# Two window-attention stages made one stream of 32 tiles each, and two expert stages reordered

## The reference, cut to what matters

```python
# window attention, DEPTH = 2 layers, HEADS = 8, DIM_HEAD = 64, WINDOW = 64
h = shift_token(x)                       # the upper 64 channels come from the token before
q, k, v = split(h @ wqkv)
q, k = l2norm(q) * qs, l2norm(k) * ks
q, k = rotary_xpos(q, k)                 # multiply by cos and sin tables
x = x + local_attention(q, k, v) @ wo    # each window of 64 sees itself and the one before
h = shift_token(x)
h = (h - mean(h)) / sqrt(var(h) + 1e-5) * lg + lb
a, g = split(h @ w1 + b1)                # 341 wide each
x = x + (a * gelu(g)) @ w2 + b2

# experts: groups of 32 tokens, 128 expert slots
logits = einsum('bntd,des->bntes', grouped, Wc) + bc + tie
perm   = (logits == max over the 32 tokens)          # each slot takes one token of a group
inner  = relu(permuted @ W1 + b1)                    # each slot has its own 128 x 32
out    = (inner @ W2 + b2), put back by perm
```

## Time and profile before

| | us |
|---|---|
| median of 3 runs | 2715.95 (2713.83 to 2716.72) |
| the profiled execution, its own time | 2716.01 |
| its span in the profile | 2714.2 |
| first window stage (377.7 to 795.3) | 417.6 |
| second window stage (837.0 to 1252.7) | 415.7 |
| first expert stage (2302.0 to 2399.5) | 97.5 |
| second expert stage, from 2607.9 to its last addition at 2705.6 | 97.7 |

### The profile page before, as it was taken

How to read it: one execution, slowest core, us unless ns; L and a number is a source line. 1 busy time by engine, 2 the same in 40 slices (tenths; PEclk the granted TensorE clock), 3 DMA queues, 4 the chain that set the end, 5 groups by cost and what they waited for, 6 DMA issues and landing times. The chain is left out here.

```text
span 2714.2 us, 42839 instructions
## 1 busy us (share of the span) xinstructions
PE 2225.2 (82%) x15196; PEld 1524.2 (56%) x15196; DVE 1772.0 (65%) x4423; ACT 1385.8 (51%) x3630; POOL 718.8 (26%) x472
## 2 busy tenths in 40 slices
PE   6999979889887987978447887768776988689978
PEld 4888846636643653653347774433424765556648
DVE  6777748759746965964656663356456997637863
ACT  3555537738734764864411226563636764326750
POOL 0000016516502642630033420000012976051000
PEclk9999999989988989999678898888987999778986
DMA  1000021100002101001012320000001221100010
GB/s 56 14 19 15 7 72 22 23 20 21 21 5 75 25 17 24 21 16 48 0 36 58 74 46 0 12 12 6 4 12 56 86 70 60 45 10 2 2 65 17
DMA packets 79043, 80.92 MB, mean 30 GB/s; under 512 B 28624, under 2 KB 63952, under 8 KB 77808
## 3 DMA queue, kind: packets, MB, share of 16 engines
q1 hardware_dynamic: 78832, 78.19, 10.1%
HBM read 53.94 MB, written 8.52 MB: 23 GB/s over the span
## 5 line engine op out<-in xcount | busy, mean ns | idle before, releaser
L1014 ACT ACTIVATE window_s<-window_s,window_soft 128x128 f32<-128x128 f32 x512 | 197.7, 394 | 5.0 <-DVE window_soft L1177 5.0
L1084 POOL TENSOR_TENSOR window_s<-window_s,window_soft 128x512 f32<-128x512 f32 x128 | 133.2, 1041 | 218.5 <-DVE window_soft L1114 218.4
L1092 POOL TENSOR_TENSOR window_pa<-window_pa,window_pb 128x1024 f32<-128x1024 f32 x64 | 151.5, 2368 | 148.8 <-DVE window_pb L1159 148.8
L1177 DVE CUSTOM_DVE_ANT_0 window_s<-ps,window_mask,window_nrn 128x128 f32<-128x128 f32 x512 | 148.7, 346 | 46.7 <-PE ps L859 29.9
L3127 DVE TENSOR_TENSOR_SCAN mamba_bx<-ps,mamba_ab 128x256 f32<-128x256 f32 x256 | 154.5, 667 | 18.9 <-PE ps L2913 18.9
L822 PE MATMUL ps<-window_wa,window_sh 128*128 128x512 f32 x256 | 131.3, 638 | 41.4 <-DVE window_pb L1159 28.4
L3297 ACT ACTIVATE rope_p<-ps,rope_mx 128x128 f32<-128x128 f32 (+1 forms) x256 | 104.3, 419 | 53.1 <-DVE rope_mx L3351 53.1
L2910 PE MATMUL ps<-mamba_m,mamba_xt 128*128 128x129 f32 x512 | 102.9, 283 | 29.6 <-ACT mamba_m L2985 20.6
L83 PE MATMUL ps<-x,consts 128*128 128x512 f32 x120 | 77.0, 801 | 46.1 <-PEq L53 40.5
L3015 POOL TENSOR_TENSOR h<-mamba_bx,mamba_cbr 128x1024 f32<-128x1024 f32 x32 | 89.3, 2796 | 93.2 <-DVE mamba_bx L3127 92.7
L2910 PEld LDWEIGHTS ps<-mamba_m,mamba_xt 128*128 128x128 f32 x512 | 82.3, 197 | 49.1 <-issue 49.1
(11 more groups left out here) (607 smaller groups left out, 6235.9 us busy)
## 6 DMA issues: line engine op xcount, KB each, us to landing
mamba_cbr<-mamba_c SPq DMA_DIRECT2D x32, 512.0 KB, 3.7
window_vs<-window_vt SPq DMA_DIRECT2D x64, 128.0 KB, 2.3
delta_xi<-delta_x SPq DMA_DIRECT2D x16, 512.0 KB, 5.1
switch_w<-in_switch_w SPq DMA_DIRECT2D x4, 2048.0 KB, 10.1
window_wa<-in_window_wa SPq DMA_DIRECT2D x4, 1152.0 KB, 6.8
linattn_wb<-in_linattn_wb SPq DMA_DIRECT2D x6, 513.0 KB, 3.5
window_wb<-in_window_wb SPq DMA_DIRECT2D x4, 537.5 KB, 7.7
window_sh<-y SPq DMA_DIRECT2D x16, 128.0 KB, 2.2
```

The source lines that it names most:

```text
L1014: a = nc.scalar.activation(s[:, k % 2, e, c, :], s[:, k % 2, e, c, :], ACT.Exp, scale=-1.0, bias=soft[:, k % 2, e, 1, c:c + 1], accum_out= ...
L1084: nc.gpsimd.tensor_tensor(s[:, k % 2, e], s[:, k % 2, e], soft[:, k % 2, e, 3, :].unsqueeze(2).to_broadcast([P, QC, P]), ALU.mult)\
L1092: nc.gpsimd.tensor_tensor(own, own, pb[:, :, :, :].rearrange("p a h d -> p (a h d)"), ALU.add)\
L1177: v = nc.vector.tensor_tensor_reduce(s[:, k % 2, e, c, :], K.ps[:, B_S + e, toks(c, P)], mask[:, k % 2, :], nrn[:, k % 4, h:h + 1], 3e38, ...
```

## The change

Attention. The 2 x 16 tiles of both layers become one stream of `N` = 32 tiles in `SLOTS` = 42 steps. The second half of a layer is divided into single uses of a bank, and each use is put into a step. `part(i)` says which: from step 8 on, r = (i - 8) mod 4 is the place in a block's cycle, b the block whose cycle it is (0 to 7 over both layers), and last = b - 1. Bank `B_V` is used once more in each step between the copy of v and the next v (`early`, and `mean` at r = 0), and `B_S` between the mask of one tile and the scores of the next (`late`). A block's two gate parts are first copied with their bias (`move_gate`), then one gelu of 1024 columns takes both; the third part has its gelu straight from PSUM. The table for gelu is loaded before and the one for exp and ln after it, once for each block (17 loads a stage, where it was 4). The shifts by DMA (`sh`, `sh2`) follow the blocks. The final block alone still writes its shifted copy by VectorE.

Experts. `z` is stored with the slot innermost. The picks come as eight units of 8 matmuls whose two banks are copied by ScalarE and VectorE side by side; the bias and the tie are added in one VectorE operation from PSUM; the copies of the transposed choice move to ScalarE; W1's moving operand becomes `z[:, :, 4q + r]`, with a step of 128 elements between its columns. In the combination the roles are exchanged: the choice (128 x 32) is the stationary operand and the result (128 columns) moves; b2 is added by four matmuls for each block; the result has tokens on the partitions and is copied (`y_tm`) and transposed back (`turn_back`). The three activities are interleaved by block.

```diff
+    N, BLOCKS = DEPTH * TILES, DEPTH * NJ
+    SLOTS = N + 10
+    FIRST = 2 * TPW
+    def part(i):
+        b, r = divmod(i - FIRST, TPW)
+        return (b if 0 <= b < BLOCKS else None), (b - 1 if 1 <= b <= BLOCKS else None), r
...
+            def early_moved(i):
+                b, last, r = part(i)
+                if r == 0 and last is not None:
+                    pe.wait_ge(st.hid_done, 3 * last + 2)
+                if r == 1 and b is not None:
+                    pe.wait_ge(st.log_ready, b + 1)
+                if r >= 2 and b is not None:
+                    pe.wait_ge(st.g_moved, 3 * b + 2 * r - 3)
...
+            def early(i):
+                b, last, r = part(i)
+                pe.wait_ge(st.v_copied, up_to(i))
...
+                if r == 0 and last is not None:
+                    hidden(last, 1)
+                if r == 1 and b is not None:
+                    var(b)
+                if r == 2 and b is not None:
+                    gate(b, 0)
+                if r == 3 and b is not None:
+                    gate(b, 2)
+
+            def late(i):
...
+                if r == 0 and last is not None:
+                    hidden(last, 2)
+                if r == 1 and last is not None:
+                    mlp_out(last)
+                if r == 2 and b is not None:
+                    gate(b, 1)
+                if r == 3 and b is not None:
+                    hidden(b, 0)
...
+            for i in stream:
+                b, last, r = part(i)
+                if 2 <= i < N + 2:
+                    turn_qk(i - 2)
+                if i < N:
+                    project_qk(i)
+                if i >= FIRST:
+                    early(i)
+                if 2 <= i < N + 2:
+                    scores(i - 2)
+                if 4 <= i < N + 4:
+                    project_out(i - 4)
+                if r == 0 and b is not None:
+                    early_moved(i)
+                    mean(b)
+                if 3 <= i < N + 3:
+                    turn_p(i - 3)
+                if i < N:
+                    project_v(i)
+                if i >= FIRST:
+                    late(i)
+                if 3 <= i < N + 3:
+                    values(i - 3)
...
+            def gelus(b):
+                m = HC[2][1]
+                act.wait_ge(st.hid_g, 3 * b + 3)
+                if b >= 1:
+                    act.wait_ge(st.hid_done, 3 * b)
+                nc.scalar.activation(gl[0:m, 2, :], K.ps[0:m, B_V, :], ACT.Gelu, bias=b1g(b // NJ, 2))\
+                    .then_inc(st.g_moved, 1)
+                act.wait_ge(st.g_moved, 3 * b + 2)
+                nc.scalar.activation(gl[:, 0:2, :], gl[:, 0:2, :], ACT.Gelu).then_inc(st.gelu_done, 1)
+                nc.scalar.preload_act_table_set("natural_log_exp_and_others")
...
-    z = st.sb("z", [P, ES, NG])
+    z = st.sb("z", [P, NG, ES])
...
+            def combine(j):
+                bank = K.ps[:, 4 + j % 2, :]
+                if j >= 2:
+                    pe.wait_ge(st.y_copied, j - 1)
+                for t in range(TPW):
+                    nc.tensor.matmul(bank[:, toks(t, P)], perm[:, toks(TPW * j + t, P)], b2, start=(t == 0), stop=False,
+                                     skip_group_check=True)
+                pe.wait_ge(st.moved_act, 2 * (j + 1))
+                pe.wait_ge(st.moved_dve, 2 * (j + 1))
+                for t in range(TPW):
+                    for g in range(4):
+                        n = 4 * (TPW * j + t) + g
+                        mm = nc.tensor.matmul(K.ps[32 * g:32 * g + 32, 4 + j % 2, toks(t, P)], perm[:, toks(n, GT)],
+                                              resm[:, n, :], start=False, stop=True, skip_group_check=True)
+                mm.then_inc(st.y_ready, 1)
```

More of the change, by code:

```diff
@@ new lines, in _ @@
+            for i in stream:
+                b, last, r = part(i)
+                if 3 <= i < N + 3:
+                    exps(i - 3, 1)
+                if 2 <= i < N + 2:
+                    move_qk(i - 2)
+                if 1 <= i < N + 1:
+                    inverse(i - 1)
+                if i < N:
+                    square(i)
+                if r == 1 and b is not None:
+                    rstd(b)
+                if r == 2 and b is not None:
+                    move_gate(b, 0)
+                if r == 3 and b is not None:
+                    gelus(b)
+                if 3 <= i < N + 3:
+                    move_p(i - 3)
+                if 2 <= i < N + 2:
+                    exps(i - 2, 0)
+                if r == 0 and b is not None:
+                    centered_square(b)
+                if r == 2 and b is not None:
+                    move_gate(b, 1)
@@ new lines, in _ @@
+            for i in stream:
+                b, last, r = part(i)
+                if 4 <= i < N + 4:
+                    move_o(i - 4)
+                if 3 <= i < N + 3:
+                    recip(i - 3, 0)
+                if 1 <= i < N + 1:
+                    move_v(i - 1)
+                    norms(i - 1)
+                if 3 <= i < N + 3:
+                    recip(i - 3, 1)
+                if 2 <= i < N + 2:
+                    negate(i - 2)
+                    mask_and_max(i - 2, 0)
+                if r == 0 and last is not None:
+                    gated(last, 1)
+                if 4 <= i < N + 4:
+                    attended(i - 4)
+                if i < N:
+                    cosines(i)
+                if r == 0 and b is not None:
+                    centre(b)
+                if 2 <= i < N + 2:
+                    mask_and_max(i - 2, 1)
+                if i < N:
+                    sines(i)
+                if r == 0 and last is not None:
+                    gated(last, 2)
+                if r == 1 and b is not None:
+                    normalise(b)
+                if r == 1 and last is not None:
+                    finish(last)
+                if r == 3 and b is not None:
+                    gated(b, 0)
@@ new lines, in pick @@
+            def pick(j, u):
+                pe.wait_ge(st.chosen_copied, j + 1)
+                if u:
+                    pe.wait_ge(st.picked_act, seen[j, 0])
+                    pe.wait_ge(st.picked_dve, seen[j, 0])
+                for t in range(TPW):
+                    for e in range(2):
+                        g = 2 * u + e
+                        rows, tile = slice(32 * g, 32 * g + 32), toks(TPW * j + t, P)
+                        mm = nc.tensor.matmul(K.ps[:, j + 4 * e, toks(t, P)], h_tm[rows, tile], perm_tm[rows, tile],
+                                              start=True, stop=True)
+                mm.then_inc(st.picked, 1)
@@ L3516, in _ @@
                             mm.then_inc(st.h2_ready, 1)
[L3517 to L3530 removed]
+            turn_result(0)
```

579 lines of the change are left out of this document (265 added, 314 removed).

## The result

The changed kernel takes 2595.57 us (median, 2594.42 to 2599.26); the kernel before, run again beside it, took 2714.89. The ratio is 0.9563, 95% interval 0.9546 to 0.9580. The forecast of 2585 lies 11 us too low.

A forecast was written before the change was run, and what follows sets the result against it. TensorE (PE) was to become the bound, where a loop over PE and ACT closed the steps. Window stages -75.7 and expert stages -55.6 sum to -131.3 from 2716.0, so 2584.7 us; range 2550 to 2630.

The forecast's parts named there:

- The walk of the four steps: Attention stream, one block: steps r = 0 to 3 of 11.35, 10.9, 9.1, 11.1 us; taken as 43.0, bounds 40 and 46.
- Rival 1: PE's order hides the waits: a block 40 us, expert stages give 34 each, 2538 us; below 2550, chance 0.10.
- rival 2: Bank uses in the stream serialise, each waiting for its reader: 12 us a step, +60, 2645 us; above 2630, chance 0.12.
- rival 4: TensorE falls to 1.2 GHz inside the stream: 38.6 us more for each such block; chance 0.02.
- rival 3: Table loads hold ScalarE longer than their own 1.28 us, lengthening r = 3: +41, 2626 us; chance 0.03.
- The stage's sum: One window stage: 76.1 + 39.6 + 215.0 + 10.5 + 37.6 = 378.8 us; both stages together minus 75.7.
- the 2.8 us: Window stage's start: first shift of y no longer waits for the last of four normalisations, 78.9 to 76.1 us.
- (a): Expert picks: two units side by side, copies 0.6 to 0.66 us, W1 beginning at 2326.7: minus 14.9 us a stage.
- DVE's queue sets the end: Expert picks: four `choose` of 2.1 us until 2321.2, then seven copies of 0.75 us, ending at 2326.5.
- (b): W1 in an expert stage: moving operand stepping 512 bytes costs +1 us on 5.86, between no cost and +5.9.
- (c): Expert stage's end, transposes and combination: 35.5 us falls to 21.6, minus 13.9.
- rival 5: Expert part fails by itself (W1 twice as long, the end at the low clock): +25, 2610 us; no chance given.

The follow-up runs named there:

- gating_before_mask: The changed kernel with VectorE doing gated(last, 1) before its first mask in steps r = 0, not after it: 2587.82 us, ratio 0.9526 to the kernel before.
- no_table_switch: The changed kernel with both gelus replaced by copies with and without bias, so the table loads fall out (output lacks the gelu): 2581.53 us, ratio 0.9503.
- expert_part_only: The kernel before with only the new expert stages (`switch_stage`), window stages as before: 2666.99 us, ratio 0.9820.
- mlp_out_one_product: The changed kernel with one of the three `mlp_out` products kept in r = 1 (two hidden parts left out): 2583.62 us, ratio 0.9514.
- both_steps_padded: The changed kernel with `z` rows of 130 (520 bytes) and results in rows of 65 (transpose weights step 260 bytes): 2595.26 us, ratio 0.9556.

## Why the prediction was right, and where it was off

**The walk of the four steps.** Predicted 11.35, 10.9, 9.1 and 11.1 from scores to scores, taken as 43.0 a block; measured 11.68, 11.06, 9.46 and 10.72, 42.9 (by the copies of v 11.68, 11.19, 9.32 and 10.72). Rival 1 (waits hidden, 40) and rival 2 (uses serialise, 12 us a step) fell by this, and rival 4 by the clock of 1.00 in the stream. The steps were right in their causes also. r = 0 waited for the gating: `gating_before_mask` took the wait away. It is smaller than drawn (0.9 us of TensorE, not the 1.1 from 2.0 to 3.1), and behind it stood the centring. r = 1 is TensorE alone, as said: it is busy all of the 11.06 us. "If `finish` came 2 us later, `v_copied` would hold the gate" was too generous: `finish` ended 7.8 us after the scores, as walked (8.0), but the copy of the output, a reciprocal and the copy of v itself follow, and `v_copied` came 1.04 us before it was needed. r = 3 was over-priced by 0.4.

**The table loads.** The row of 1.28 us back to back held in the new place: 1.28, gelu 0.02 later, 0.02 from the second gelu to the second load, 0.01 from its end to the copy. The Trainium skill's page "ScalarE: Activation LUTs", section "What ACT_TABLE_LOAD costs", adds about 1380 ns of drain to a switch; no such gap is in these rows, and rival 3 fell. The page's advice to batch by set (section "Table sets: the hidden batching unit") still has a price here: 1.38 us a block. Not 16 blocks pay it: from the scores of step 8 to those of the last tile a stage lost 8.0 us, and the chain at its end, which had a stretch at the lower clock in this run, got no shorter. So it is 16 us by the steps, and 14 by the medians (no_table_switch 2581.5, the change 2595.6).

**The stage's sum.** 380.7 and 379.5 for 378.8, by terms (both stages, from scores to scores): the start 78.5 and 77.3 for 76.1, the first block 39.9 and 39.9 for 39.6, the five full blocks 214.0 and 214.0 for 215.0, step 32 10.4 for 10.5, the chain at the end 37.9 for 37.6. The start is the term that was mis-sized. The first copy of v came 1.3 us earlier, nearer the first stage's start, but most of the lead was gone at the next one (7.48 us later, where it had been 6.55; here a stretch at the lower clock lay from 396.9 to 403.7, before from 390.2 to 397.0). From the stage's start to the copy of tile 7 it was 77.1 us for 77.4 before, and in the second stage 75.9 for 76.5. Of the 2.8 us 0.3 and 0.6 were left. Even these can't be told from chance: in other traces the same code took 75.7 to 79.0 for this stretch, and the code of before 76.4 to 79.8.

**The expert stages.** Predicted -27.8 each, measured -18.0 and -24.6. (a) The picks: W1 began 10.1 us earlier in the first stage and 14.7 in the second, for 14.9. The copies were 0.60 and 0.69 side by side as said, so the failed part is "DVE's queue sets the end". The last units, first stage:

```profile
2249.44 6.07 PE L3536 MATMUL ps<-ln_xc,ln_sq 32*128 32x128 f32 x64
...
2255.54 0.60 ACT L3617 ACTIVATE switch_z<-ps 128x512 f32<-128x512 f32 x1 [1.33 <-PE ps L3536]
2255.54 0.69 DVE L3677 COPY switch_z<-ps 128x512 f32<-128x512 f32 x1 [1.23 <-PE ps L3536]
```

Both copying engines wait for TensorE, at a clock of 0.55. Four units take 6.07 us, 1.5 each, where I let copies of 0.75 set the pace. Part of that is not the clock. Before, the products of four row groups of 32 stood side by side in TensorE's order; four records, one for each row group, then came every 0.21 us at the lower clock and every 0.11 at the higher. A unit has two row groups, and mostly only two records come in the same 0.21 or 0.11. A set of 32 records at the lower clock before, for comparison:

```profile
2332.64 2.09 PE L3494 MATMUL ps<-ln_xc,ln_sq 32*128 32x128 f32 x32 [3.12 <-DVE switch_z L3453]
```

The prediction has no term for TensorE in the picks, and no run prices this pairing alone. In the second stage the picks lay at the higher clock; the last copies began 25.7 us after the stage's start, not 28.6, and the gain is nearly the predicted one.

(b) W1 is the step that failed: "between no cost and twice its length (+5.9) I take +1", by the ratio of the transposes whose weights step 256 bytes. It measured 12.5 us, +6.7 in the first stage and outside the bound, and 10.2, +4.3, in the second; in four other kernels the same code took 10.2 to 10.9, inside the bound. A ratio for weights that step 256 bytes said nothing of a moving operand that steps 512. With 516 bytes my +1 would have been +1.9. I had "W1's moving operand at several times its time" as a sign of being wrong; it was about twice.

(c) The end took 22.0 us (from the first transpose to the last addition) for 21.6, at a clock of 0.91: right, and -13.5 for -13.9; 21.8 in the second stage.

Together: the window stages gave 2.6 us less than forecast, the expert stages 13.0 less, and the untouched stretches returned 4.3 that nobody had forecast: 2.6 + 13.0 - 4.3 = 11.3, the distance from 2584.7 to the profiled execution (span 2594.2 and 1.8 around it). That the untouched stages took 4.3 off the miss is luck. Of rival 5 (expert part fails by itself, 2610) half came true, by its first cause.

What stays open: why the same stretches differ between the traced executions, and how VectorE comes to be slow beside W1. Adds over 0.7 us came only with a step of 512 bytes: there the first add of a stage took 0.77 to 2.83 us, and in the first stage here the next two 1.58 and 1.14, while with 516 or 520 bytes and contiguous all took 0.68 to 0.69. The lower clock isn't needed, since the 1.58 and the 1.14 lie wholly at the higher one; which of the two memories is contended isn't shown. Nor was the exchange of roles in the combination tried by itself, so what of the 13.5 us is the exchange, the interleaving or the clock is not shown.

## What to carry to other kernels

Walk a software pipeline step by step with durations from its own trace, and in each step name the second to last arrival too: here a wait that was taken away gave 0.65 of 0.85 us, and work that was taken away 0.9 of 1.7, because another engine stood just behind. When a layout is turned so that copies write unbroken rows, look at what then reads it with a step, and try one element more in each row of 128 fp32; it costs 256 bytes of each partition here, and the two expert stages took 152.1 us with it, 157.1 to 161.2 without. Read small differences by the length of the stage that was edited, not by the whole time.

## What the runs showed of the hardware

**A moving operand with a step.** Time of one W1 product's pass (64 columns; two records a product, 256 in all), from their spacing: contiguous 0.014 us at TensorE's higher clock and 0.026 at the lower (both in the kernel before); 516 bytes apart 0.029 at either; 520 bytes 0.031 at either; 512 bytes 0.037 to 0.046 at the higher and 0.045 to 0.053 at the lower. A padded step thus costs about twice the contiguous time at 2.4 GHz and a tenth more at 1.2 GHz, as if the operand came at a fixed rate of its own. That is why W1 took 7.8 us with 516 bytes at whatever clock. The 6.2 and 8.1 us of the contiguous form hold 0.9 and some 3 us of pauses, so they are no measure of the two clocks.

**Weights with a step.** A transpose took 0.146 us with weights 256 bytes apart, 0.123 with 260 and 0.109 with contiguous ones, at the higher clock; at the lower, 0.213 in all three. The rule that the prediction quotes from the Trainium skill ("SBUF — State Buffer", "Door 1: The DMA port swizzle") would price steps of 256 and 260, of 512 and 516 alike, since each element lies in a line of its own; the runs separate them.

**Untouched stages are not constant.** In the table above the stretch from delta to mamba, whose code is the same in all kernels, lasts from 714.9 to 723.0 us, and the one between the expert stages from 201.8 to 208.4, while mamba to experts varies by 0.1 among the kernels with the new stream, and is 2.3 us shorter in the two without it. The changed kernel's own expert stages took 161.2 us together and the same code 157.1 to 158.0 in four others, with the granted clock falling at other places. Each program was traced in one execution, so it isn't shown whether the program or the execution decides; the runs of one program lay up to 8 us apart (expert_part_only, mlp_out_one_product) or within 1.5 (both_steps_padded). A difference of 5 us between two programs is within that, however narrow the interval of each ratio.
